# A twelve-sublayer decoder with two expert layers: expert weights fetched by SyncE, later expert rows held back, one ScalarE table set

## What is computed

```python
x = x + _L0_attn_ref(_layernorm(x), ...)      # 0: rope attention and SwiGLU
x = x + _L0_xattn_ref(_layernorm(x), ...)     # 1: cross attention, 16 heads of 8
x = x + _L0_ffn_ref(_layernorm(x), ...)       # 2: Sinkhorn-routed experts, top 2 of 8
x = x + _L1_attn_ref(_layernorm(x), ...)      # 3: flow attention
x = x + _L1_xattn_ref(_layernorm(x), ...)     # 4
x = x + _L1_ffn_ref(_layernorm(x), ...)       # 5: quantised FFN
x = x + _L2_attn_ref(_layernorm(x), ...)      # 6: ReLU attention
x = x + _L2_xattn_ref(_layernorm(x), ...)     # 7: attention with 16 heads of 64
x = x + _L2_ffn_ref(_layernorm(x), ...)       # 8: softmax-routed experts, top 2 of 8
x = x + _L3_attn_ref(_layernorm(x), ...)      # 9: block-wise causal linear attention
x = x + _L3_xattn_ref(_layernorm(x), ...)     # 10
x = x + _L3_ffn_ref(_layernorm(x), ...)       # 11: int8 FFN
```

## Time and profile before

| | |
|---|---|
| three runs | 1977.89, 1985.57, 1986.81 us |
| the profiled execution | 1987.53 us, its span 1985.7 us |
| busy share of the span | PE 74%, DVE 62%, ACT 47%, POOL 19% |
| sublayer 2 (Sinkhorn experts) | about 407 to 586 us of the span |
| sublayer 3 (flow) | 587 to 746 us |
| sublayer 8 (experts) | up to 1644 us |
| sublayer 9 (block) | 1644 to 1768 us |

### The profile page before, as it was taken

One profiled execution on the slowest core, in us unless ns is written; L12 is line 12 of the kernel. 1 busy time (PEld: TensorE's weight loads), 2 busy tenths in 40 slices (PEclk: granted clock), 3 DMA queues, 4 the chain that ended last, 5 costly groups with the idle time before them and its releaser, 6 DMA issues. The chain is left out here.

```text
span 1985.7 us, 32127 instructions
## 1 busy us (share of the span) xinstructions
PE 1468.4 (74%) x11270; PEld 894.7 (45%) x11270; DVE 1222.3 (62%) x4051; ACT 934.6 (47%) x2009; POOL 380.2 (19%) x404
## 2 busy tenths in 40 slices
PE   5997978844763669996446599999974993677874
PEld 2554434433551443443224356666654882443432
DVE  7776378844233647776666477777664223557876
ACT  4554266642221235554632177777752440126655
POOL 3320021013645005320011000000002546002100
PEclk9999999965995779999557599999995995669995
DMA  3320023112451003320010000000003662003300
GB/s 117 57 44 2 0 34 48 23 32 64 140 120 36 1 26 64 52 44 19 0 55 1 11 6 7 6 7 12 1 8 91 203 182 56 1 16 44 54 2 21
DMA packets 58686, 84.52 MB, mean 43 GB/s; under 512 B 8352, under 2 KB 46496, under 8 KB 58016
## 3 DMA queue, kind: packets, MB, share of 16 engines
q1 hardware_dynamic: 48384, 46.54, 11.5%
q0 software_dynamic: 10144, 35.93, 6.4%
HBM read 51.18 MB, written 9.18 MB: 30 GB/s over the span
## 5 line engine op out<-in xcount | busy, mean ns | idle before, releaser
L638 DVE TENSOR_REDUCE maxs<-ps 128x4 f32<-128x1024 f32 x192 | 234.8, 1223 | 62.5 <-PE ps L966 60.9
L794 ACT ACTIVATE L_xattn_probs<-ps 128x1024 f32<-128x1024 f32 x192 | 196.5, 1024 | 85.1 <-PE ps L991 80.8
L3386 ACT ACTIVATE wide_pr<-wide_sc,wide_nm 128x256 f32<-128x256 f32 x256 | 126.9, 497 | 12.7 <-DVE wide_nm L3321 12.2
L966 PE MATMUL ps<-keys,L_xattn_qs 64*128 64x256 bf16 x768 | 75.3, 274 | 38.4 <-DVE maxs L638 31.9
L1007 PE MATMUL ps<-L_xattn_probs,values 128*32 128x256 f32 x1536 | 102.8, 385 | 0.0
L3293 DVE CUSTOM_DVE_ANT_0 wide_sc<-ps,wide_mask 128x256 f32<-128x256 f32 x256 | 93.8, 420 | 9.6 <-PE ps L3411 8.6
L3316 DVE COPY wide_prT<-ps 128x512 f32<-128x512 f32 x64 | 44.3, 692 | 83.0 <-PE ps L3424 82.8
L1484 POOL DMA_INDIRECT moe_xs<-normed,moe_table x92 | 86.8, 944 | 28.0 <-issue 28.0
L991 PE MATMUL ps<-L_xattn_qm,keys 64*128 64x256 bf16 x768 | 74.6, 271 | 7.3 <-ACT L_xattn_probs L794 7.0
L1890 DVE SCALAR_TENSOR_TENSOR moe_z_sb<-ps,moe_wt,moe_a_sb 128x256 f32<-128x256 f32 x46 | 22.3, 484 | 89.8 <-ACT moe_a_sb L1922 77.1
L3331 DVE TENSOR_SCALAR wide_pr<-wide_pr,wide_inv 128x256 f32<-128x256 f32 x256 | 75.5, 349 | 1.8
(11 more groups left out here) (641 smaller groups left out, 3798.5 us busy)
## 6 DMA issues: line engine op xcount, KB each, us to landing
keys<-L_xattn_k_parts SPq DMA_DIRECT2D x108, 64.0 KB
L_xattn_qs<-L_xattn_q_parts SPq DMA_DIRECT2D x108, 64.0 KB
expert_out<-moe_y SPq DMA_DIRECT2D x46, 128.0 KB
weights<-in_packed_L_xattn SPq DMA_DIRECT2D x2, 1316.0 KB, 7.5
keys<-L_attn_k_parts SPq DMA_DIRECT2D x36, 64.0 KB
L_attn_qs<-L_attn_q_parts SPq DMA_DIRECT2D x36, 64.0 KB
normed<-moe_xn SPq DMA_DIRECT2D x2, 1024.0 KB, 4.8
wide_mask<-in_mask SPq DMA_DIRECT2D x8, 256.0 KB, 2.8
```

The lines of the kernel that those rows point to most:

```text
L638: v.tensor_reduce(nm, ps[:, BANK_M:BANK_M + 2, :].rearrange("p j (t n) -> p j t n", t=2), AX.X, ALU.max, negate=True).then_inc(S("m_used"), 1)
L794: a.activation(probs[:, s % RING, :, :, :].rearrange("p j t n -> p j (t n)"), ps[:, BANK_P:BANK_P + 2, :], ACT.Exp, scale=HD ** -0.5)\
L966: mm = pe.matmul(ps[:, BANK_M + j, c + c0:c + c1], qs[half[j], m % 2, gp, q0:q0 + P], kk[half[j], m % 2, gp, b * SEQ + c0:b * SEQ + c1], s ...
L3386: ins = a.activation(pr[:, s % 3, j, qt, :], sc[:, s % 2, j, qt, :], ACT.Exp, bias=nm[:, s % 2, n:n + 1], accum_out=sums[:, s % 2, n:n + 1])
```

## The change

Three things change.

1. In both expert stages the weights of a slice are no longer fetched by POOL's indirect DMA. SP reads the slice's row number from SBUF into a register and issues a plain DMA of 128 consecutive rows from there. It issues the first four once `rows_of` is ready, and those of slice j+4 right after the store of `y` of slice j. POOL's list keeps only the rows, which wait as before for `x_turned`.
2. ACT's list of the Sinkhorn stage begins with a load of the table set that has both exp and ln.
3. In flow and block POOL waits before the fetches of the third pair (m = 2) for a point of the first pair, and before those of the fourth for the same point of the second: `scaled` in flow, the fourth `kv_ready` in block.

```diff
@@ class Sorting
     def fetch(self, g):
         C, S = self.C, self.C.sem
-        def weights(j):
-            if j >= BUFS:
-                g.wait_ge(S("y_ready"), j - BUFS + 1)
-            g.indirect_dma_start(self.wt[:, j % BUFS, :], None, self.experts,
-                                 bass.IndirectOffsetOnAxis(self.rows_of[:, j:j + 1], 0))\
-             .then_inc(C.routed[f"w_loaded_{j % BUFS}"], 16)
-
-        def rows(j):
+        g.wait_ge(S("normed_stored"), 16)
+        g.wait_ge(S("table_ready"), 1)
+        for j in range(SLICES):
             if j >= BUFS:
                 g.wait_ge(S("x_turned"), j - BUFS + 1)
             for h in range(HALVES):
...
-        g.wait_ge(S("rows_ready"), 1)
-        weights(0)
-        g.wait_ge(S("normed_stored"), 16)
-        g.wait_ge(S("table_ready"), 1)
-        rows(0)
-        weights(1)
-        rows(1)
-        for j in range(2, SLICES):
-            weights(j)
-            rows(j)
+    def weights(self, sp, j):
+        row = sp.value_load(self.rows_of[0:1, j:j + 1], min_val=0, max_val=7 * P)
+        sp.dma_start(self.wt[:, j % BUFS, :], self.experts[bass.ds(row, P), :])\
+          .then_inc(self.C.routed[f"w_loaded_{j % BUFS}"], 16)
 
     def keep(self, sp):
         C, S = self.C, self.C.sem
+        sp.wait_ge(S("rows_ready"), 1)
+        for j in range(BUFS):
+            self.weights(sp, j)
         for j in range(SLICES):
             sp.wait_ge(S("y_ready"), j + 1)
             sp.dma_start(C.expert_out[...], self.y[:, j % 2, :]...)
+            if j + BUFS < SLICES:
+                self.weights(sp, j + BUFS)
@@ sinkhorn_moe
             def _(a):
+                a.preload_act_table_set("natural_log_exp_and_others")
                 centre_odd(a, C, xn, shift)
@@ flow_attention
                     for m in range(PAIRS):
+                        if m >= 2:
+                            g.wait_ge(sem(m - 2)("scaled"), 1)
                         tail.fetch(g, m)
@@ block_attention
                     for m in range(PAIRS):
+                        if m >= 2:
+                            g.wait_ge(sem(m - 2)("kv_ready"), 4)
                         tail.fetch(g, m)
```

## The result

The changed kernel takes 1935.26 us (median of 4 runs, 1930.36 to 1936.15); the kernel before, four runs by now, 1982.32. The ratio is 0.9753, interval 0.9729 to 0.9778. The profiled execution took 1935.21 us, 52.3 less than that of before; the forecast was 1936.

A forecast was written before the change was run, and what follows sets the result against it. The prediction saw a chain through every stage, each with its own limit: PE in sublayer 8, POOL's fetches in sublayer 2, flow and block. Terms summed to -51.4, so 1987.5 became 1936 us, range 1922 to 1965.

The forecast's parts named there:

- Table set, -6.9: Sinkhorn rounds: bare table loads go, 2.22 us in each of three rounds and 0.2 for the last Exp.
- Sublayer 2's loop, -19.9: Slices step at PE's own 3.60 us instead of a mean 4.55 once SP fetches the weights: -19.9 us.
- Sublayer 8's loop, 0: PE bounds its slices; weights take some 9.5 us against 9.6 available, so no cost and no steady-state gain.
- The loop starts, -1.5 and -1: Start of sublayers 2 and 8: slice 1's rows come 2.5 us earlier; range -2.5 to +3 each.
- Flow, -14.5: Flow's first pair reaches `scaled` 16.8 us sooner without two late handovers, less 2.3 kept back.
- block, -12.6: Block's key-value step comes 14.6 us sooner, less 1 us each for late rows of pairs 2 and 3.
- the 2.3 held back: Flow's first pair: reserve because 16 fetches end only 3 us before the first handover.
- The bursts of eight, +5: Flow and block: two runs of eight fetches each delay PE's handovers, 1.25 us times four.
- The first and second: Rivals: short bursts stall like the long one (1977, chance 0.12); flow and block's standstill has another cause (1960, 0.10).
- The third: Rival: weights become sublayer 2's wait, giving back 8.6 to 15 us of 19.9; 1945 to 1951, chance 0.13.
- The table set was kept: Against the rival that the Sinkhorn stage's table set is not kept: 1943 us, chance 0.04.
- The slower one: Rival: SP's chain closes both expert loops, slower than before from 13 us on, some 2010 at 15; chance 0.03.

The follow-up runs named there:

- changed_again: The changed kernel run once more, nothing altered, on another chip: 1928.36 us, ratio 0.9952 to the kernel before there.
- stagger: The changed kernel with the first four expert weights spread behind the first two slices' turned rows: 1925.03 us, ratio 0.9943 to the kernel before there.
- hold_alone: The kernel before with only the third and fourth pairs' fetches held in flow and block: 1953.33 us, ratio 0.9845.
- spaced: The changed kernel without held fetches; GpSimd clears a 128x512 tile before each fetch of the second to fourth pairs: 1929.75 us.
- joined_thin: The changed kernel with first weights spread, sublayer 2's next weights before the y store, and 8-column clears before fetches instead of holds: 1919.37 us.
- joined_held: The changed kernel with first weights spread, sublayer 2's next weights before the y store, and one earlier wait in block: 1921.55 us.

## Why the prediction was right, point by point

The three mechanisms were right, on a chip of the first sort. That the sum came out to half a microsecond is luck.

- **Table set, -6.9: right to the hundredth**, and alone as in the whole. The bare stretches were counted from rows, and no drain of 1380 ns beside each load shows in the result either.
- **Sublayer 2's loop, -19.9: right, -18.5.** The step is 3.60. The missing 1.4 are the two slices that wait for weights (0.79 + 0.89), less 0.19 for a short first step. SP's timeline of after shows the price that was taken blind: 0.74 to 0.91 us, once 1.1, from the end of the y store's issue to the weights' issue, the register read among it (1 was taken).

```profile
483.35 0.38 SPq L1496 DMA_DIRECT2D expert_out<-moe_y  x1
484.48 0.34 SPq L1485 DMA_DIRECT2D moe_wt<-in_packed_experts  x1
486.77 0.38 SPq L1496 DMA_DIRECT2D expert_out<-moe_y  x1
488.00 0.24 SPq L1485 DMA_DIRECT2D moe_wt<-in_packed_experts  x1
```

  The weights landed 3.6 us after their issue (median of 19 in changed_again; 4 was taken). The margin of half a microsecond was real, and it is gone where the gathers are slow.
- **Sublayer 8's loop, 0: right, with a slip in the working.** By the prediction's own terms the chain from a result to the next weights is not 9.5 but 10.1 us (4 x 1.84 = 7.4 for the transfer), more than the 9.6 there are. It didn't matter, since 707 KB landed in 4.4 us (median in changed_again), and issues on SP took 0.2 to 0.4 us as a rule, not 0.66.
- **The loop starts, -1.5 and -1: the wrong sign, +1.2 and +2.4**, inside the bounds of +3. The step that failed is "slice 1's rows come 2.5 us earlier from POOL": they were asked for earlier and landed later (by 0.3 us in sublayer 2, 1.8 in sublayer 8), and slice 0's, which the prediction left out, landed 1.2 and 2.7 us later, for SP's four transfers were beside them. stagger shows it.
- **Flow, -14.5, and block, -12.6.** Until `scaled` flow gained 18.2, so the 2.3 held back weren't needed, and the sums ran shorter as well (PE L2194 1.97 us at a granted clock of 1.00; 3.43 at 0.57 before, after PE had been idle for 9.55 us). The prediction had no term for the clock. Block's key-value step came 15.6 sooner (14.6 said). The handovers that it calls late by up to 4.9 us after the last fetch are flow's; block's came 5.1 us after (1690.61 less 1685.47).
- **The bursts of eight, +5: too much.** Behind the `scaled` of the first pair flow lost 1.0 us (104.3 against 103.3 from the first totals to the last add), block 2.7 with its late rows, for which 2 stood beside the 2.5. Together 3.7 in place of 7. These are net of the clock: flow as a whole was granted 0.71 in place of 0.68; in hold_alone, with 0.68 as before, flow lost 1.8.
- **Rivals.** The first and second fell: no handover is stalled by a run of eight, and none is late while POOL is silent. The third came true in two slices, at a fifth of its lower price. The table set was kept. The slower one was far off.

The sum is right to half a microsecond since its errors offset each other: +6.1 at the two starts and +1.4 in the loop against -3.7 in flow's first pair, -1.0 in block's and -3.3 at the bursts.

What the prediction didn't see is that its result holds for one sort of chip. On the chip of changed_again the kernel before takes 1937.72 and the changed one 1928.36: 0.5%, hardly more than the table set's 6.9 us. The held fetches give back 30 us in flow and block, and 45 to 47 are missing in the kernel before there, so that sublayer 2's loop must be fast there too; its "remote" idle time (ACT 10.7 us in five waits, one of which is in the earlier trace rows) would then be the same ailment. That is argued and not shown: there is no profile of the kernel before from such a chip. Its mean granted clock there (0.857 and 0.860, medians of 18 and 28 runs; 0.849 on two chips of the first sort) is near the changed kernel's (0.856 to 0.860), which agrees with it and no more.

Open therefore: whether the standstill comes by number or by rate (spaced and joined_thin ran where there was none to take away), what distinguishes the chips, and whether joined_thin keeps its lead over the changed kernel on a chip that stalls. There joined_held, which keeps flow's later runs at eight, is likely the safer one; it too was timed on one chip only.

## What to carry to other kernels

Where an engine's work comes late with a release that no row explains, look at what GpSimd issues beside it: breaking a run of 32 indirect fetches into 16, 8 and 8 at a point of the consumer cost 1 to 3 us a stage and gave 13 to 17 net, on chips of the first sort. Ask for a loop's first rows before its first weights: four prefetches that nobody needs yet cost 2 to 4 us at each start. Time a change of a few per cent on more than one chip, the kernel before beside it, before its cause is told.

## What was unexpected of the hardware

- Chips differ, or their states at different times: the same kernel took 1983 to 1985 us on two chips and 1934 and 1938 on two others, each in one session, while sublayer 8's 22 steps took 104.8 us on all.
- On the first sort, what comes from PE, and DVE's signals to itself, are late from about the thirteenth to fifteenth indirect DMA that GpSimd issues 1.25 us apart: 0.35 to 1.3 us for DVE's self-wait (up to 1.5 later in the run), 5.8 to 10.0 us from PE to ACT and up to 15.1 us from PE to DVE, in place of 0.04, until 1.2 to 5.2 us after the last issue has ended. From ACT to PE it was 0.05 us in the same stretch of before.
- Row gathers in the last slices of sublayer 2 held the DMA engines three times as long per byte as those in the middle (41.8% of their time for 0.28 MB in 13 us, 22.8% for 1.32 MB in 38).
